# A one-core language-model tower: token halves with their own norm, router and expert tiles, and a first stage in three slices

## What is computed

```
h  = W[x] + positions                                  # gather of 2048 rows
h  = h + proj(linear attention(norm(h)))               # 8 heads, elu(q)+1, elu(k)+1
x  = norm(h)
x  = x + wo(causal softmax attention(rms(x)*ln1))      # 4 heads, 2 kv heads, rotary tables
f  = rms(x) * ln2                                      # one norm over each token
p  = softmax(f @ router.T);  top 2 of 8, renormalised  # the router
y  = x + sum_e weights[:, e] * (silu(f @ w1[e].T) * (f @ w3[e].T)) @ w2[e].T
h  = h + y                                             # then a norm, a Toeplitz (Fourier) mixer
                                                       # with a position network, a linear layer
```

## Time and profile before

| | |
|---|---|
| median of 3 runs | 367.31 us |
| lowest, highest | 366.73, 368.72 us |
| the profiled execution | 368.48 us, span 366.7 us |
| TensorE busy | 323.0 us (88%) |
| VectorE busy | 237.2 us (65%) |
| ScalarE busy | 144.1 us (39%) |
| GpSimd busy | 105.4 us (29%) |
| chain that ended last | TensorE 66%, VectorE 15%, ScalarE 6%, GpSimd 5% |

### The profile page before, as it was taken

How to read it: one execution, slowest core, us unless ns; L and a number is a source line. 1 busy time by engine, 2 the same in 40 slices (tenths; PEclk the granted TensorE clock), 3 DMA queues, 4 the chain that set the end, 5 groups by cost and what they waited for, 6 DMA issues and landing times.

```text
span 366.7 us, 4601 instructions
## 1 busy us (share of the span) xinstructions
PE 323.0 (88%) x1703; PEld 180.6 (49%) x1703; DVE 237.2 (65%) x398; ACT 144.1 (39%) x238; POOL 105.4 (29%) x137
## 2 busy tenths in 40 slices
PE   1256988987999999979999999999999999899995
PEld 0122665552433434656754555555555555467734
DVE  0578678878998740357784555553856677745385
ACT  2022416460586686521554445553450120012250
POOL 5787000236321223200002422221004878700000
PEclk9997899999999999989899999999999999999998
DMA  7939500068000000000000000000000000000001
GB/s 257 321 103 419 216 2 0 0 118 143 2 3 0 4 2 1 2 0 2 0 1 2 0 0 3 0 0 2 1 2 0 0 2 0 0 0 3 0 0 59
DMA packets 6168, 15.29 MB, mean 42 GB/s; under 512 B 1282, under 2 KB 3714, under 8 KB 5506
## 3 DMA queue, kind: packets, MB, share of 16 engines
q1 hardware_dynamic: 5583, 14.45, 12.8%
q0 software_dynamic: 512, 0.53, 0.6%
q10 hardware_dynamic: 51, 0.01, 0.0%
HBM read 12.05 MB, written 0.52 MB: 34 GB/s over the span
## 4 chain that ended last, share of the span: by engine, by line
PE 66%; DVE 15%; ACT 6%; POOL 5%; issue 4%; DMA 2%; SPq 1%; DVEq 0%; POOLq 0%; ACTq 0%
PE ps L299 64%; POOL e_lo L426 2%; DVE arena L1485 1%; DMA idt<-ident 1%; DMA arena<-arena 1%; DVE share L1278 1%; DVE xc L1242 1%; DVE st L1234 1%; DVE st L1241 1%; DVE sq L1250 1%; POOL arena L492 1%; DVE rw L1416 1%; ACT L989 1%; PE ps L506 1%; ACT sq L983 1%
## 5 line engine op out<-in xcount | busy, mean ns | idle before, releaser
L1416 DVE TENSOR_REDUCE rw<-ps 128x1 f32<-128x512 f32 (+2 forms) x80 | 45.7, 629 | 7.6 <-PE ps L299 7.2
L299 PE MATMUL ps<-bfc_s 128*128 128x512 bf16 (+2 forms) x201 | 49.2, 358 | 0.0
L1102 ACT ACTIVATE arena<-ps 128x1024 f32<-128x1024 f32 (+3 forms) x48 | 37.6, 812 | 29.0 <-PE ps L299 28.6
L299 PE MATMUL ps<-arena 96*128 96x512 bf16 (+7 forms) x192 | 43.0, 328 | 1.4 <-DMA arena<-arena 0.8
L299 PE MATMUL ps<-xs,e_hi 128*128 128x512 f32 x96 | 40.6, 423 | 0.6 <-ACT arena L1128 0.6
L1485 DVE TENSOR_TENSOR arena<-ps,arena 128x512 f32<-128x512 f32 x48 | 33.1, 691 | 11.2 <-ACT arena L1128 10.8
L1128 ACT ACTIVATE arena<-ps 128x512 f32<-128x512 f32 x48 | 28.6, 597 | 26.3 <-PE ps L299 22.6
L299 PE MATMUL ps<-xs,e_lo 128*128 128x512 f32 x96 | 38.6, 402 | 0.0
L299 PE MATMUL ps<-share,tu_s 128*128 128x384 f32 x96 | 32.5, 488 | 0.0
L299 PEld LDWEIGHTS ps<-arena 96*128 96x128 bf16 (+1 forms) x192 | 15.8, 98 | 29.0 <-DVE rw L1416 13.2
L299 PEld LDWEIGHTS ps<-bfc_s 128*128 128x128 bf16 x201 | 20.2, 101 | 17.9 <-issue 2.5
(11 more groups left out here) (237 smaller groups left out, 491.5 us busy)
## 6 DMA issues: line engine op xcount, KB each, us to landing
arena<-arena SPq DMA_DIRECT2D x24, 96.0 KB, 2.8
w<-wpack SPq DMA_DIRECT2D x1, 2152.5 KB
arena<-tm SPq DMA_DIRECT2D x2, 1024.0 KB, 5.8
arena<-epack SPq DMA_DIRECT2D x1, 1540.0 KB, 11.4
arena<-rope SPq DMA_DIRECT2D x1, 1024.0 KB
tu_s<-tu SPq DMA_DIRECT2D x2, 512.0 KB, 12.4
tk_s<-tk SPq DMA_DIRECT2D x2, 512.0 KB, 13.9
rp<-rpack SPq DMA_DIRECT2D x1, 678.5 KB, 4.5
```

Of the source, the lines that this page charges most:

```text
L299: return nc.tensor.matmul(o, l, r, start=start, stop=stop, **kw)
L1102: nc.scalar.activation(pt[:, n % PT_SLOTS, :, lo:512], ps[:, bank:bank + 2, lo:512], ACT.Exp, scale=HD ** -0.5).then_inc(S("exp_done"), 1)
L1416: V.tensor_reduce(top_view(m, part)[:, at:at + len(heads), i], src, AXX, ALU.max, negate=True).then_inc(S("ring_read"), 1)
```

## The change

1. First stage: the gathers, `embed` and the centring go in three slices of 4, 2 and 2 blocks, set between the layers of the position network; its last `normalise` and the filling of `geo` come after the k products. The ones in `kst` come by two DMAs instead of a memset. `keep_warm(7)` becomes `keep_warm(2)`.
2. GpSimd: `e_lo` in four pieces, set between its copies of q and k pieces; the `wst`, `wpc` constants and the bias pieces move to `late_constants`, in the middle of attention.
3. The norm, the transposes, the router's products and its top 2 go by halves. The upper half comes first, its norm before the last projection; `keep_warm(34)` goes. The lower half's norm is between the expert tiles (transposes after tile 10, router products after the first `down_duo`, its exp after silu 16, its weights before `down_duo` 4). The tiles run upper halves first. One root is a power on GpSimd, and GpSimd adds `x1` to `h`.

```diff
+SLICES = ((0, 4), (4, 6), (6, 8))
+LOW_CUTS = (1048, 1560, 2584)
+TILES = ((0, 1), (1, 1), (0, 0), (1, 0))
+LOW_NORM_TILE = 10
+LOW_LOGITS_DUO = 0
+LOW_EXP_TILE = 16
+LOW_ROUTE_DUO = 4
-ORDER += [("o", 1, 0), ("y", 1, 0), ("yT", 0, 0), ("o", 0, 0)]
+ORDER += [("o", 1, 0), ("y", 1, 0), ("yT", 0, 0), ("norm", 1, 0), ("o", 0, 0)]
...
@@ gpsimd
-            nc.gpsimd.memset(kst[MROW:KROWS], 1.0).then_inc(S("constants"), 1)
...
+            pool.wait_ge(S("qmin"), 1)
             nc.gpsimd.memset(va2[:], 0.0).then_inc(S("constants"), 1)
...
+            duplicate(0)
+            duplicate(1)
+            pool.wait_ge(S("q_pieces"), 1)
+            pool.wait_ge(S("k_pieces"), 1)
...
+            split_low(0, LOW_CUTS[0])
+            duplicate(2)
+            pool.wait_ge(S("e_high"), 3)
+            pool.wait_ge(S("e_low"), 1)
+            split_low(LOW_CUTS[1], LOW_CUTS[2])
+            pool.wait_ge(S("q_pieces"), 2)
...
                 elif kind == "cols":
+                    if x == UNIT_END[1]:
+                        late_constants()
                     diagonal(x)
...
+            pool.wait_ge(S("mean_squares"), NORMS["var2b_lo"])
+            nc.gpsimd.tensor_tensor(st[:, 4, 0:8], st[:, 2, 0:8], powers[:], ALU.pow).then_inc(S("roots"), 1)
+            pool.wait_ge(S("roots"), NORMS["rms2b_lo"])
+            nc.gpsimd.tensor_tensor(h[:], h[:], x1[:], ALU.add).then_inc(S("residual"), 1)
@@ tensor
-                    keep_warm(7, 7)
+                    keep_warm(2, 7)
...
-            keep_warm(34, 7)
...
+            pe.wait_ge(S("yT"), len(COL_UNITS))
+            pe.wait_ge(S("e_low"), 4)
+            logits(1)
...
+                    if 3 * n + n3 == LOW_NORM_TILE:
+                        pe.wait_ge(S("ring_read"), RING_LAST[6])
+                        norm_transposes(0, (5, 6))
                     if DUOS[n, n3] is not None:
+                        if DUOS[n, n3] == LOW_ROUTE_DUO:
+                            pe.wait_ge(S("wb"), 2 * LOW_ROUTE_DUO)
+                            weight_transposes(0, 7)
                         down_duo(DUOS[n, n3])
+                        if DUOS[n, n3] == LOW_LOGITS_DUO:
+                            pe.wait_ge(S("wb"), 2 * LOW_LOGITS_DUO + 2)
+                            logits(0)
                 if n == LAG - 1:
-                    pe.wait_ge(S("wpc"), 3)
...
+                    pe.wait_ge(S("xs"), 4)
+                    weight_transposes(1, 6)
@@ scalar
+                    if m == LOW_NORM_TILE + 1:
+                        norm_copies(0, (5, 6))
+                    if m == LOW_EXP_TILE:
+                        next_function(ACT.Exp)
+                        router_exp(0)
+                        next_function(ACT.Silu)
+                    if DUOS[n, n3] == LOW_ROUTE_DUO:
+                        act.wait_ge(S("wT"), 2)
+                        nc.scalar.copy(wst[0:96, 0:512], ps[0:96, 7]).then_inc(S("wst"), 1)
@@ vector
+            logit_rests(1)
+            to_gate(1)
+            dve.wait_ge(S("constants"), CONSTANTS["wpc_zero"])
+            choose(1, next_gate)
+            norm_rows(0)
+            next_gate()
+            norm_split(0)
+            to_gate(13)
+            logit_rests(0)
+            to_gate(LOW_EXP_TILE + 2)
+            choose(0, next_gate)
+            to_gate(3 * ALL_PAIRS - 1)
```

More of the change, by code:

```diff
@@ L137 @@
 ORDER += [("pv", _p, 0) for _p in range(_pairs, len(PV_BEHIND))]
[L138 removed]
+ORDER += [("o", 1, 0), ("y", 1, 0), ("yT", 0, 0), ("norm", 1, 0), ("o", 0, 0)]
 assert not _todo
[L140 removed]
+RING_ORDER = [x for x in ORDER if x[0] not in ("cols", "pv", "norm")]
+RING_LAST = {bank: max(n for n in range(len(RING_ORDER)) if RING_BANKS[n % 3] == bank) + 1 for bank in RING_BANKS}
 WCOLS = {}
@@ L414, in _ @@
-            step(nc.gpsimd.tensor_tensor(left[64:96], left[64:96], uvb[64:96], ALU.subtract))
-            nc.gpsimd.tensor_copy(uvb[64:96], left[64:96]).then_inc(S("bias_pieces"), 1)
-            pool.wait_ge(S("constants"), CONSTANTS["k_ones"])
-            for n, (pcs, (first, end, by), value) in enumerate(((pieces_q0, Q_SLOTS[0], 1), (pieces_k, K_SLOTS[0], 2),
-                                                                (pieces_q1, Q_SLOTS[0], 5))):
+            for a, (lo, hi) in enumerate(SLICES):
+                pool.wait_ge(gathered[a], 16 * B * (hi - lo))
@@ L1300, in _ @@
             scale_rows(sq, xc, 4, S("n1"))
-            normalise(LAYERS)
             evac(3, S("T1"), 2, S("xT1_hi"))
+            dve.wait_ge(S("r_rms"), LAYERS + 1)
+            step(V.tensor_scalar(rh[:, 2], rh[:, 2], 1e-8, None, ALU.add))
+            step(V.reciprocal(rh[:, 2, 0:P], rh[:, 2, 0:P]))
             dve.wait_ge(S("xT1_lo"), 1)
@@ L1526, in _, with to_gate @@
-            for n in range(ALL_PAIRS):
-                for n3 in range(3):
-                    if gates[0] <= 3 * n + n3:
-                        gate()
+            def to_gate(m):
+                while gates[0] <= m:
+                    n, n3 = gates[0] // 3, gates[0] % 3
+                    gate()
                     if DUOS[n, n3] is not None:
```

406 lines of the change are left out of this document (240 added, 166 removed).

## The result

The changed kernel takes 377.2 us (median of 4 runs, 375.98 to 377.63), the kernel before, on the same chip, 368.0 us (4 runs, 366.73 to 368.79). The ratio is 1.025, 95% interval 1.022 to 1.029: slower by 9.2 us. Forecast was slower, but by 4.3 us, and the 377.2 lies above the range's end of 376.5.

A forecast was written before the change was run, and what follows sets the result against it. TensorE was taken to bound attention, VectorE the stretch to the first product back at 192.21. Terms -3.3 -0.8 +1.6 +0.3 +1.2 +1.8 +2.2 +1.3 gave +4.3 us: 371.6 us, own range 369.3 to 374.3, 8 in 10 365.0 to 376.5.

The forecast's parts named there:

- Part 6: Between the expert tiles, TensorE full there: router's products +1.8, table loads +2.2, wait before `down_duo` 4 +1.3 us.
- part 1, first stage: First stage: slices and no memset bring centring and k/v products earlier, net -3.3 us, bounds -4.5 and -0.5.
- part 2, `top_pieces`: GpSimd ahead of attention: early `e_lo` pieces let `top_pieces` start earlier, -0.8 us, bounds -1.8 and 0.
- part 3, constants: In attention: the moved constants delay the third `top_pieces`, for which TensorE waits, +1.6 us, bounds 0 and +2.5.
- parts 4 and 5, head start and clock: Residual to first `down_duo`: 7.0 us head start used up by VectorE's work, +0.3, and low clock after a wait, +1.2 us.
- part 6, router's products: Between the tiles: the lower half's router products fall where TensorE is full, +1.8 us.
- part 6, table loads: Behind silu 16: two table loads and the exp block ScalarE 3.1 us ahead of the `wb` copy, +2.2 us.
- VectorE's router work beside the gates: Lower half's choice on VectorE between the tiles: no term in the sum, so 0 us.
- part 6, ahead of `down_duo` 4: Before `down_duo` 4: TensorE waits for the transposed weights, silu 31 and a copy, +1.3 us, bounds 0 to 2.
- rival d: First stage: slices wait for the gathers anyway, only the memset's 1.3 us is gained, 373.6 us; with the forecast 0.52.
- Rival (a): First gate to first `down_duo`: head start survives, that `down_duo` under 34.5 us after the residual; 363.5 to 366.3 us; chance 0.20.
- rival (c): Tiles: low clock twice, table loads in full, VectorE held up behind GpSimd's sums one to three times; 374 to 378 us; 0.14.

The follow-up runs named there:

- e3_exp_beside_down: The changed kernel with the lower half's exp and its two table loads behind the `wb` copies of `down_duo` 1: 373.9 us, ratio 1.017.
- e8_ones_dma: The kernel before with only the ones in `kst` by DMA instead of GpSimd's memset, no slices: 365.4 us, ratio 0.996.
- e1_slices: The kernel before with the change's first stage, early `e_lo` and constants in attention; norm, router and experts whole: 365.6 us, ratio 0.9945.
- e2_slices_consts: e1_slices with the constants and bias pieces behind GpSimd's first `top_pieces`: 363.5 us, ratio 0.989.
- e4_low_norm_first: The changed kernel with the lower half's norm ahead of the upper half's choice, its transposes behind tile 4 instead of 10: 371.5 us, ratio 1.010.
- e5_warm: The changed kernel with 14 filler products on TensorE in the 3.79 us wait behind tile 10: 371.4 us, ratio 1.012.
- e10_spread: e9_all_warm with the lower half's choice of experts begun one gate earlier and spread over more gates: 364.9 us, ratio 0.993.
- e7_all_wt: The changed kernel with lower norm first, exp behind `down_duo` 1, constants behind first `top_pieces`, lower weights' transposes one tile earlier: 367.4 us, ratio 0.998.
- e9_all_warm: e7_all_wt with 14 filler products on TensorE ahead of the transposes of the upper half's norm: 364.7 us, ratio 0.991.
- e11_best: The kernel of e2_slices_consts run again unchanged: 364.2 us, ratio 0.991.

## Why the prediction was right and wrong

The sign was right, and so was the mechanism of most terms; the size was half. Two steps of the prediction failed where it mattered. Part 6 priced the table loads at their wait alone, 2.2 us, and they cost 3.9; and its "TensorE is full there" charged nothing for the lower half's router work on VectorE, which cost 1.4. These are 3.1 of the 4.4 us that the sum lacked. By the trace, term by term:

| term | forecast | measured | from |
|---|---|---|---|
| part 1, first stage | -3.3 | -2.95 | copy of the context |
| part 2, `top_pieces` | -0.8 | -0.4 | 3.38 less 2.95 |
| part 3, constants | +1.6 | +1.6 | what is left of 3.38 at the residual, 1.79 |
| parts 4 and 5, head start and clock | +1.5 | +1.9 | residual to last products of `down_duo` 0, 41.4 - 39.5 |
| part 6, router's products | +1.8 | +1.8 | `down_duo` 0 to 1 in e3_exp_beside_down |
| part 6, table loads | +2.2 | +3.9 | the other 2.3 of `down_duo` 0 to 1, and 1.6 of 1 to 2 |
| VectorE's router work beside the gates | 0 | +1.4 | `down_duo` 2 to 3 |
| part 6, ahead of `down_duo` 4 | +1.3 | +1.4 | `down_duo` 3 to 4 |
| sum | +4.3 | +8.7 | |

**Part 1** came out right for a wrong reason, and the nearness of -2.95 to -3.3 is partly luck: the eleven traces with this first stage have the copy of the context 2.9 to 4.7 us earlier than before. The step that failed is "after the gathers and the third `normalise`, which a slice ahead of it puts at about 25.2": a slice ahead of it puts it later, since VectorE works in order and that slice waits for its gathers. What gave the 2.95 us is the memset that is gone, which was priced at 1.3 (rival d); e8_ones_dma has 3.3 us at the same row from it alone. In the traces it is worth over twice its own 1.3, because TensorE is then not at the low clock, at which the earlier trace rows has it at 36 to 38 us.

**Part 2.** In the trace the `e_lo` piece from 71.23 to 73.63 does hold up VectorE, whose instruction with both inputs in SBUF takes 1.85 us where its like takes 0.69, while the one ahead of it, with one input in PSUM, takes its usual 0.68:

```profile
71.23 2.40 POOL L425 TENSOR_TENSOR e_lo<-arena,e_hi 128x1048 fp32r<-128x1048 f32 x1 [1.28 <-DVE arena L1514]
...
71.61 0.68 DVE L1502 TENSOR_TENSOR tmp<-ps,arena 128x512 f32<-128x512 f32 x1
72.32 1.85 DVE L1504 TENSOR_TENSOR share<-share,tmp 128x512 f32<-128x512 f32 x1
```

The second piece (76.42 to 78.77) does the same to one from 77.58, 1.73 us. The Trainium skill's rule (SBUF — State Buffer, "SBUF: two separate sides"), that the second waits for the first one's whole instruction, agrees with this trace in both places; its result of 0 for the part was as near to the measured -0.4 as the -0.8 taken.

**Part 3** held: +1.6 in the trace, and 1.4 to 2.1 us back when the constants moved (e1_slices against the two sets of e2_slices_consts).

**Parts 4 and 5** held as a mechanism: TensorE waits 3.79 us after tile 10 (forecast: 4) and the first `down_duo` comes 38.9 us after the residual (36 to 39). The 41.4 us to its last products are those of one execution: e3_exp_beside_down, which has the same instructions up to there, took 42.8, with a granted clock of 0.50 at 184 to 193 us where the change has 0.62. What was wrong is to call this the price of VectorE's work, 14.6 us of it. e4_low_norm_first has the same work and takes 6.2 us less, 3.6 of them apart from the clock. It was the order: the norm stood behind the choice, so that the row norm, transposes, silu, copies, transposes and three tiles after it had nothing beside them. Rival (a) asked for under 34.5 us at that place and got 38.9. With the order mended the first `down_duo` comes 32.7 us after the residual, so (a)'s condition holds; its time, 363.5 to 366.3, does not (371.5), since the loads and the router work are still to be paid.

**Part 6, the loads**, is the term that was mis-sized the most: +2.2 in the sum, +3.9 measured. The wait is 2.3 us, as forecast (2.2); the clock behind it, 1.6 us, was not in the sum, though rival (c) had it. e3_exp_beside_down and e5_warm take the two apart: the one removes both, but for 1.5 us at the next `down_duo`, the other the clock alone. The Trainium skill's drain of 1380 ns (ScalarE: Activation LUTs, "What ACT_TABLE_LOAD costs") does not show here: the next instruction starts 1.29 us after either load does, and the block from 201.40 to 204.46 is 3.06 us, the 3.1 of the sum without a drain.

**The missing term** is VectorE at `down_duo` 2 to 3. Part 6 said "TensorE is full there", and nothing was charged for the 24 small instructions of the lower half's choice. 18 of them stand between `down_duo` 2 and 3, beside six gates and two `weigh`. VectorE is busy for 8.91 us there, of the 10.67 that the period takes, where the period before had 5.44 of 9.29; and TensorE is only three tiles ahead and waits for a gate (0.55 us at 218.55). One of the 18 takes 1.16 us instead of 0.23, beside a sum of GpSimd that starts just before:

```profile
216.13 1.30 POOL L516 TENSOR_TENSOR sq<-sq,arena 128x512 f32<-128x512 f32 x1
...
216.35 1.16 DVE L1651 TENSOR_TENSOR rw<-w,st 128x64 f32<-128x64 f32 x1
...
218.55 0.50 PE L308 MATMUL ps<-xs,e_hi 128*128 128x512 f32 x1 [0.55 <-DVE arena L1620]
```

That is what (c) feared, "one to three times": it is twice (again at 226.50, 0.94 us instead of 0.21). How much of the 1.4 us is this hold-up and how much the work itself, no run separates; spreading the work over more gates (e10_spread) moved the loss and did not remove it. Of (c)'s three conditions two came true, the second low clock and the hold-ups, these at 0.7 to 0.9 us a time instead of 1.3; the loads did not show in full. Its range of 374 to 378 holds the time. It had 0.14; the low clock behind a second wait deserved more, since the earlier trace rows showed two such places.

**Part 6, ahead of `down_duo` 4**, held: TensorE waits 1.02 us for the copy of the transposed weights (+1.4 over the interval, forecast +1.3), and e7_all_wt, which has the copy one tile earlier, gets 0.9 of it back in its trace.

```profile
232.31 0.38 PE L308 MATMUL ps<-wst,bfc_s 128*128 128x512 bf16 x1 [1.02 <-ACT wst L1223]
```

**Do the halves pay once repaired?** e7_all_wt and e2_slices_consts add the high half's residual at the same 151.42 us. At `down_duo` 0 the halves are 2.6 us ahead (186.87 against 189.46), at 1 0.8 ahead, at 2 0.7 behind, at 3 2.3, at 4 2.8 and at the last 2.8 behind. The head start is smaller than what is paid for it: 1.8 us of router products between the tiles, 1.5 for the loads, 1.6 for the choice, 0.5 for the transposes of the weights. With fillers in the wait ahead of the upper half's transposes (e9_all_warm, 364.7) they draw level with the kernel without halves (e11_best, 364.2) and do not pass it. The best found is that kernel: the change without its halves, its constants behind the first `top_pieces`, in two sets 363.5 and 364.2 us, about 1% under the kernel before. Not tried: the fillers of e9_all_warm and e5_warm together, the order of the tiles and the add on GpSimd by themselves, and the halves without slices.

## What to carry to other kernels

Splitting work to start earlier buys a head start only if what the second part needs first stands first in its engine's order: here two moved calls, with the transposes six tiles earlier, were worth 5.7 us, in the traces 3.6 for the order itself and the rest for the clock that no longer fell. Price each new wait of TensorE twice, once for the wait and once for the clock behind it, and look for ScalarE's table loads next to a copy that TensorE is about to need; the same loads behind that copy cost 1.5 us instead of 3.9. An instruction "off the path" on GpSimd can sit on it through VectorE: by the copy of the context, removing one 3.5 us memset gave the stage all that its redesign in slices did.

## What the runs showed of the hardware

- The same wait of 2.23 us did not always lower TensorE's clock. In the change, where the granted clock had been 0.62 from 184 to 193 us, it fell again behind the wait at 203 us; in e5_warm and e4_low_norm_first, with 1.00 at 184 to 193 us, it stayed at 1.00 behind it. What decides it these runs don't show.
- What the clock costs behind one wait differs between executions: from the eight transposes behind tile 10 to the last products of `down_duo` 0 it took 8.4 us at a granted clock of 1.00 at 184 to 193 us (e5_warm), 10.7 at 0.62 (the change) and 12.2 at 0.50 (e3_exp_beside_down).
- Runs of one kernel differ by up to 4.5 us with the clock: e4_low_norm_first at a mean granted clock of 0.989 took 367.7 us, at 0.968 372.0 and 372.2. e9_all_warm, with fillers ahead of the upper half's transposes, had 0.995 in all five runs, within 1.6 us.
- GpSimd's power of 128x8 values took 1.68 us where its subtraction of 128x8 takes 0.20 (L501 against L474). It cost nothing here, as the norm that needs it came 12 us later.
